# The moment matmuls of an output slot are moved from the slot's end to the place before the projection

## The chip, the cores and the metric

The kernel runs on one core of one Trainium2 chip. The time is the device time of one execution in microseconds (us). TensorE multiplies matrices and writes to PSUM; VectorE, ScalarE and GpSimd work element by element; SyncE issues DMAs. Each engine executes its own list of instructions in order, and engines wait for each other by semaphores that only count upwards.

## The reference

The model takes `x` of 16 images, 64 x 64 positions (4096 tokens), 128 channels in float32. Layer 0 is a group norm and a two-dimensional LSTM. Layer 1 is Nystrom attention with 8 heads and 64 landmarks over the tokens, and then a recurrence with a batch norm in front of it. What matters here is the end of the attention and what the recurrence needs of it:

```python
out = attn1 @ attn2_inv @ (attn3 @ v)            # per head
out = out + res                                  # res: a convolution of v along the tokens
t = t + (x + out @ w_out + b_out)                # x: layer norm of the tokens
t = t + _L1_ffn_ref(_ln_t(t), W, V, gamma, beta)

# in _L1_ffn_ref
Wx = einsum('bti,hi->bth', x, W); flat = Wx.reshape(B * T, H)
Wx = (Wx - mean(flat)) * rsqrt(var(flat) + BN_EPS) * gamma + beta
```

The mean and the variance of `Wx` go over all tokens of all images. The kernel gets them from the sums and the second moments of the normalised tokens, which are ready only when the last token has been through the attention.

## The kernel before, in words

The phases run one after another: group norm, LSTM, landmarks, pseudo-inverse, output, recurrence. The change touches the output phase (`output_phase`). It works on 16 images of 8 chunks (`NG`), 512 tokens each, one chunk to a slot: 128 slots. `each_image` calls an engine's `slot(b, c, ...)` for image `b` and chunk `c`; there is a `slot` per engine, and the order of the calls in it is that engine's order of work, written out by hand. There is no planner. The work on one chunk is spread over several slots, so a slot also handles chunks c+1 to c+3 (ahead) and c-1 to c-4 (behind).

TensorE's slot (L2229), in order:

- `scores(c)` (L2171, L2175): into four PSUM banks; it waits among others for ScalarE's copy of the last convolution, because `bank_conv` is one of the four
- `row_maxima(c+1, 0)` (L2152): the approximate scores of the first half of the next chunk into two banks; VectorE reduces each bank (`maxima`, L2355), and the second call waits for those reductions before it writes the banks again
- `project(c-3)` (L2211): the output projection, into `bank_x`
- `row_maxima(c+1, 1)` (L2152): the second half
- `weigh(c)` (L2185): waits for ScalarE's four exponentials (L2318)
- `queries(c+3)` (L2138), `turn_maxima(c+1)` (L2160), `convolve(b+1, c)` (L2197), `turn_convolved(c-2)` (L2205)
- `moments(c-4)` (L2224): 16 small matmuls of the normalised tokens `u` with themselves, summed in `bank_m` over all slots

VectorE's slot (L2399): the four reductions for chunk c+1 (L2355), `residual(c-3)` (L2366), which adds the projection to the base and takes layer norm statistics of the result (L2369, L2372), `reciprocals(c-1)` (L2386), `normalise(c-2)` (L2397), `add_convolved(c-2)` (L2380), `merge(c-1)` (L2391).

GpSimd's slot (L2099): `mask(c-1)` (L2073), `norm(c-3)`, `base(c-1)` (L2097). `norm` waits for the statistics of the residual, adds epsilon (L2082, here called the variance step), raises to the power -0.5 (L2084) and multiplies the residual by it into `u` (L2089, the product). `u` has two buffers, taken in turn. `norm(c-3)` is called in slot c, so its result is what `moments(c-4)` of slot c+1 reads. SyncE stores each `u` to the tensor `scaled` and moves the softmax sums to packed form and back (L1987, L1996, L2003).

ScalarE's slot (L2314): exponentials (L2318), half of the base scaling (L2302), copies of queries, weighed values and maxima (L2295, L2310, L2312, L2280, L2284), the copy of the convolution (L2289), the other half of the scaling.

After the last slot the remaining `project`, `turn_convolved` and `moments` calls run down one by one, and ScalarE copies `bank_m` out when all moments are done (L2343).

Of the kernel before, what the change touches and what calls it, by code (L numbers as in the profile page):

```python
# [1877 lines left out]
def output_phase(nc, sems, R, E, K, xnt, tokens, vals, recips, scaled):  # L1878


    with ExitStack() as ctx:
# [47 lines left out]
        def nth(b, c):  # L1929

            return NG * b + c + 1

        def wait(eng, name, count):

            if count > 0:
                eng.wait_ge(s[name], count)
# [13 lines left out]
        def follows(c, k, last):  # L1950

            return c + k < NG or not last

        def precedes(c, k, first):

            return c >= k or not first
# [171 lines left out]
        def _(pe):  # L2128
# [5 lines left out]
            def queries(b, c):  # L2134

                pe.wait_ge(*loaded(s_xl, *at(b, c)))
                wait(pe, "qc", nth(b, c) - 1)
                nc.tensor.matmul(bank_q[:, :], w[:, :], xnT[c % 4][:, :], start=True, stop=True).then_inc(s["qm"], 1)  # L2138

            def row_maxima(b, c, r, q):  # L2140

                if r == 0:
                    wait(pe, "ql", nth(b, c))
                    wait(pe, "setup", SETUP * (b + (c == NG) + 1))
                    wait(pe, "neg", nth(b, c) - 1)
                for k in range(2):
                    for half in range(2):
                        if k == 0:
                            wait(pe, "max", GT * (nth(b, c) - 1) + 2 * r + half - 1)
                        rows, heads = slice(LM * half, LM * half + LM), slice(PAIRS_H * half, PAIRS_H * half + PAIRS_H)  # L2150
                        token = P * (2 * r + k)
                        ml = nc.tensor.matmul(bank_l[half][:, 2 * P * k:2 * P * k + 2 * P], q_lp[c % 2][rows, token:token + P],  # L2152
                                              kb_lp[q][rows, heads, :].rearrange("c h l -> c (h l)"), start=True, stop=True)
                        if k == 1:
                            ml.then_inc(s["lp"], 1)

            def turn_maxima(b, c):
                wait(pe, "max", GT * nth(b, c))
                for k in range(GT):
                    mt = nc.tensor.matmul(bank_l[0][:, P * k:P * k + P], m1[:, k, :], E.ident_lp[:, :], start=True, stop=True)  # L2160
                mt.then_inc(s["mt"], 1)

            def scores(b, c, q):

                wait(pe, "neg", nth(b, c))
                wait(pe, "denc", 2 * (nth(b, c) - 1))
                wait(pe, "qc", min(nth(b, c) + 2, B * NG))
                wait(pe, "convc", min(NG + nth(b, c) - 1, B * NG))
                for g in range(PAIRS_H):
                    rows = slice(QUAD * g, QUAD * g + QUAD)  # L2170
                    nc.tensor.matmul(bank_s[g][:, :], ind[rows, :, :].rearrange("c a l -> c (a l)"), negm[c % 2][rows, :],  # L2171
                                     start=True, stop=False)
                for g in range(PAIRS_H):
                    rows = slice(QUAD * g, QUAD * g + QUAD)
                    ms = nc.tensor.matmul(bank_s[g][:, :], kb[q][rows, :, :].rearrange("c a l -> c (a l)"), qT[c % 4][rows, :],  # L2175
                                          start=False, stop=True)
                ms.then_inc(s["s1"], 1)

            def weigh(b, c, q):

                wait(pe, "exp", PAIRS_H * nth(b, c))
                for h in range(2):
                    rows = slice(LM * h, LM * h + LM)
                    for g in range(PAIRS_H):
                        mp = nc.tensor.matmul(bank_pv[h][QUAD * g:QUAD * g + QUAD, :], zb[q][rows, g, :], p1[g][rows, :],  # L2185
                                              start=True, stop=True)
                mp.then_inc(s["pv"], 1)

            def convolve(b, c, out):

                half, pair = c // GT, c % GT
                pe.wait_ge(s_v[half], 128 * (b + 1))
                turns = out.rearrange("p (n e) -> p n e", e=2 * DH)
                for a in range(2):
                    h = 2 * pair + a
                    for side in range(2):
                        mm = nc.tensor.matmul(turns[LM * side:LM * side + LM, :, DH * a:DH * a + DH], bands[:, h, :],  # L2197
                                              v[half][side][:, :, (DH + 1) * h:(DH + 1) * h + DH], start=True, stop=True,
                                              skip_group_check=True)
                mm.then_inc(s["conv"], 1)  # L2200

            def turn_convolved(b, c, q):
                wait(pe, "res", nth(b, c) - 1)
                for k in range(GT):
                    mt = nc.tensor.transpose(bank_x[:, k, :], res[q][:, GT * (c % NG) + k, :], R.ident[:, :])  # L2205
                mt.then_inc(s["ct"], 1)

            def project(b, c):
                wait(pe, "add", nth(b, c))
                for k in range(GT):  # L2210
                    mt = nc.tensor.matmul(bank_x[:, k, :], oT[:, P * k:P * k + P], wo[:, :], start=True, stop=True)  # L2211
                mt.then_inc(s["wo"], 1)

            def moments(b, c):

                n = nth(b, c)
                wait(pe, "u", n)
                if n == 1:
                    pe.wait_ge(K.ready, K.PARTS + 2)
                    wait(pe, "centre", 2)  # L2220
                for k in range(GT):
                    for g in range(P // QUAD):
                        r = (g - k) % BLOCK_ROWS
                        mm = nc.tensor.matmul(bank_m[QUAD * g:QUAD * g + QUAD, FROM[r]:FROM[r] + WIDTH[r]],  # L2224
                                              u[c % 2][:, k, 1 + QUAD * r:1 + QUAD * r + QUAD], u[c % 2][:, k, 0:WIDTH[r]],
                                              start=n == 1 and k == 0, stop=n == B * NG and k == GT - 1, skip_group_check=True)
                mm.then_inc(s["moments"], 1)

            def slot(b, c, q, first, last):  # L2229
                scores(b, c, q)  # L2230
                nq = q if c + 1 < NG else 1 - q
                if follows(c, 1, last):
                    row_maxima(b, c + 1, 0, nq)
                if precedes(c, 3, first):
                    project(b, c - 3)
                if follows(c, 1, last):
                    row_maxima(b, c + 1, 1, nq)
                weigh(b, c, q)
                if follows(c, 3, last):
                    queries(b, c + 3)  # L2240
                if follows(c, 1, last):
                    turn_maxima(b, c + 1)
                if not last:
                    convolve(b + 1, c, bank_conv[:, :])
                if precedes(c, 2, first):
                    turn_convolved(b, c - 2, q if c >= 2 else 1 - q)
                if precedes(c, 4, first):
                    moments(b, c - 4)

            nc.tensor.matmul(bank_m[:, 0:C], E.avg[:, :], fw[:, :], start=True, stop=True).then_inc(s["centre"], 1)  # L2250
            pe.wait_ge(s_band, 16)
# [8 lines left out]
            turn_maxima(0, 0)  # L2260
            wait(pe, "convc", NG)
            each_image(pe, slot)
            project(B - 1, NG - 3)
            turn_convolved(B - 1, NG - 2, 1)
# [594 lines left out]
```

## Time and profile before

| | |
|---|---|
| median of 3 runs | 5903.51 us (5903.4 to 5907.3) |
| the profiled execution, its own time | 5913.64 us |
| its span in the profile | 5911.8 us |
| TensorE matmuls busy | 5253.6 us, 89% |
| VectorE / ScalarE / GpSimd busy | 3071.2 (52%) / 3138.0 (53%) / 1523.0 (26%) us |
| scores of the output phase's first and last slot start | 2530.7 and 3561.8 us |
| last moment matmul starts | 3592.7 us |

The profile gives start and duration of each instruction on each engine. Engine names: PE is the matmul part of TensorE and PEld its weight loads, DVE is VectorE, ACT is ScalarE, POOL is GpSimd. Matmuls are pipelined, their ends are modelled and overlap the next start, so distances are best taken from start to start.

### The profile page before, as it was taken

The page shows a single profiled execution, that of the slowest core. Times are in us where ns is not written, and L with a number is a line of the kernel's source. Part 1 is how long each engine was busy: PE and PEld are TensorE (multiplying, and loading weights), DVE is VectorE, ACT ScalarE, POOL GpSimd, SP SyncE. Part 2 cuts the span into 40 slices and gives each one's busy share as a digit, 9 for nine tenths or more (in the row PEclk, how much of TensorE's full clock was granted, in tenths as well). Part 3 has the DMA queues.
Part 4 walks back from the last instruction along what each step waited for, and adds up shares of the span by engine and source line. Part 5 has one row for each costly group of instructions (what it writes and reads, how often), then busy time and mean ns, then how long its engine had stood idle before and what let it go on. Part 6 is the DMA issues. An engine that isn't in the chain of part 4 may idle for free. (4 is left out here: it accounts for less than half of the span.)

```text
span 5911.8 us, 223297 instructions
## 1 busy us (share of the span) xinstructions
PE 5253.6 (89%) x97395; PEld 3278.2 (55%) x97488; DVE 3071.2 (52%) x8152; ACT 3138.0 (53%) x9108; POOL 1523.0 (26%) x1905
## 2 busy tenths in 40 slices
PE   5599999997899998799999997888888888888888
PEld 4599888896566666744444444333333333333333
DVE  8677777775788886568888883111111111111111
ACT  6465555565677776378888883333333333333333
POOL 2100000002888874256666662000000000000000
PEclk7899999999999999999999998999999999999999
DMA  9631111225777773467777762111111111111100
GB/s 389 270 115 58 58 58 60 84 77 183 245 245 243 231 243 105 102 175 203 202 203 202 204 173 66 33 34 32 32 34 33 32 32 35 32 32 32 35 18 24
DMA packets 773031, 689.32 MB, mean 117 GB/s; under 512 B 67056, under 2 KB 663024, under 8 KB 767984
## 3 DMA queue, kind: packets, MB, share of 16 engines
q1 hardware_dynamic: 754672, 575.39, 32.6%
q0 software_dynamic: 14672, 95.16, 4.0%
q8 instruction: 743, 12.17, 0.9%
q10 hardware_dynamic: 2736, 4.89, 0.2%
q14 instruction: 208, 1.70, 0.1%
HBM read 392.17 MB, written 274.89 MB: 113 GB/s over the span
## 5 line engine op out<-in xcount | busy, mean ns | idle before, releaser
L2797 ACT ACTIVATE f_y<-f_acc 128x16 f32<-128x16 f32 x4096 | 754.7, 184 | 1542.5 <-PE f_acc L2739 1542.5
L2739 PEld LDWEIGHTS f_acc<-f_y,f_vT 128*32 128x32 f32 x32768 | 645.2, 108 | 1438.7 <-ACT f_y L2797 1437.0
L2739 PE MATMUL f_acc<-f_y,f_vT 128*32 128x16 f32 x32768 | 1046.1, 193 | 279.6 <-issue 1.5
L2697 PE MATMUL f_junk<-f_idle 128*32 128x512 bf16 x8400 | 832.5, 376 | 0.0
L2579 DVE COPY f_zT<-f_zt 128x512 f32<-128x512 f32 x124 | 85.8, 692 | 1138.4 <-PE f_zt L2653 1138.4
L2355 DVE TENSOR_REDUCE o_m<-o_bank_l 128x8 bf16<-128x512 f32 x512 | 329.7, 686 | 132.4 <-PE o_bank_l L2152 130.0
L2572 DVE TENSOR_SCALAR f_wxn<-f_wxp,f_scale,f_shift 128x512 f32<-128x512 f32 x126 | 102.1, 811 | 509.0 <-PE f_wxp L2667 508.9
L1299 ACT ACTIVATE a_p<-a_s 128x512 f32<-128x512 f32 x502 | 259.3, 602 | 153.0 <-PE a_s L1166 151.2
L2318 ACT ACTIVATE o_p<-o_bank_s 128x512 f32<-128x512 f32 x512 | 264.4, 602 | 142.0 <-PE o_bank_s L2175 142.0
L533 POOL DMA_DIRECT2D hidden<-l_h x46 | 34.7, 756 | 1162.1 <-DVE l_hsum L790 961.6
L712 ACT ACTIVATE l_gate<-l_pf,r_ctx 128x256 f32<-128x256 f32 (+7 forms) x512 | 202.5, 446 | 229.1 <-PE l_pf L643 228.8
L2592 DVE SCALAR_TENSOR_TENSOR f_sum<-f_u,f_std,f_turned 128x128 f32<-128x128 f32 x512 | 143.6, 344 | 317.9 <-PE f_turned L2690 317.9
L2697 PEld LDWEIGHTS f_junk<-f_idle 128*32 128x32 bf16 x8400 | 250.0, 99 | 0.0
L1359 DVE TENSOR_REDUCE a_m3p<-a_s 128x1 f32<-128x512 f32 x360 | 223.6, 684 | 50.8 <-PE a_s L1126 49.4
L633 PE MATMUL l_pio<-l_x,r_k_lm 128*128 128x256 f32 (+7 forms) x1024 | 239.0, 356 | 0.2 <-ACT l_gate L729 0.2
L633 PE MATMUL l_pf<-l_x,r_k_lm 128*128 128x256 f32 (+7 forms) x1024 | 238.9, 356 | 0.0
L647 PE MATMUL l_pio<-l_hsum,r_ctx 128*128 128x256 f32 (+7 forms) x1024 | 238.8, 356 | 0.0
L2302 ACT ACTIVATE o_base<-o_base,r_loss,r_gain 128x128 f32<-128x128 f32 x512 | 225.8, 498 | 0.3 <-DMA o_base<-tokens 0.3
L2690 PE MATMUL f_turned<-f_ident,f_y 128*32 128x128 f32 x4096 | 221.1, 290 | 0.5 <-DVE f_sum L2592 0.5
L1017 POOL TENSOR_TENSOR a_r<-a_vare,a_half 128x8 f32<-128x8 f32 x128 | 209.6, 1638 | 10.0
L712 ACT ACTIVATE l_gate<-l_pio,r_ctx 128x256 f32<-128x256 f32 (+7 forms) x512 | 203.4, 450 | 13.9
L2679 PE MATMUL f_acc<-f_wxn,f_ident 128*32 128x128 f32 x4096 | 207.1, 274 | 0.7 <-issue 0.7
(323 smaller groups left out, 11517.6 us busy)
## 6 DMA issues: line engine op xcount, KB each, us to landing
o_v<-vals SPq DMA_DIRECT2D x256, 272.0 KB, 3.4
a_hid<-hidden SPq DMA_DIRECT2D x112, 520.0 KB, 5.0
hidden<-l_h POOLq DMA_DIRECT2D x46, 1040.0 KB, 6.6
l_x<-skew SPq DMA_DIRECT2D x46, 1024.0 KB, 5.2
vals<-a_v SPq DMA_DIRECT2D x128, 272.0 KB, 3.4
gn_x<-in_x SPq DMA_DIRECT2D x16, 2048.0 KB, 17.4
a_xin<-in_x SPq DMA_DIRECT2D x128, 256.0 KB, 5.1
tokens<-a_t SPq DMA_DIRECT2D x128, 256.0 KB, 3.4
```

Source lines behind the costliest of these rows:

```text
L633: mm = nc.tensor.matmul(banks[c][g][:, :, rows], w[W[g]], xs, start=g in (0, 2, 3), stop=False, skip_group_check=True)
L647: mm = nc.tensor.matmul(banks[c][g][:, :, rows], w[U[g]], hsum[:, lanes[c], rows], start=False, stop=True, skip_group_check=True)
L712: nc.scalar.activation(gate[:, g, lanes[c], rows], banks[c][g][:, :, rows], ACT.Tanh if g == 2 else ACT.Sigmoid, bias=bias[BI[g]]).then_in ...
L1299: nc.scalar.activation(p3[c % 2][g][:, :], score_bank(i, c, g), ACT.Exp).then_inc(s["exp"], 1)
L1359: nc.vector.tensor_reduce(m3p[:, g, c:c + 1], bank[:, :], AX.X, ALU.max).then_inc(s["mx"], 1)
L2302: nc.scalar.activation(bs[c % 4][:, k, :], bs[c % 4][:, k, :], ACT.Identity, scale=R.gain[:, b, n:n + 1], bias=R.loss[:, b, n:n + 1]).then ...
L2318: nc.scalar.activation(p1[g][:, :], bank_s[g][:, :], ACT.Exp).then_inc(s["exp"], 1)
L2355: nc.vector.tensor_reduce(m1[:, 2 * r:2 * r + 2, LM * half:LM * half + LM].rearrange("p k (g r) -> p k g r", r=QUAD)[:, :, :, 0:2], bank_l ...
L2690: mt = nc.tensor.matmul(turned[g % 2][rows, b % 4, :], y[q][:, rows, b], ident[:, :], start=True, stop=True)
L2697: nc.tensor.matmul(junk[rows, :], idle[:, 0:QUAD], idle[:, :], start=True, stop=True)
L2739: mm = nc.tensor.matmul(acc[k % 2][rows, t, :], vT[:, rows], before, start=False, stop=True, skip_group_check=True)
L2797: nc.scalar.activation(y[q][:, step, :], acc[step // RC % 2][:, step % RC, :], ACT.Sigmoid).then_inc(s_y, 1)
```

## The change

In TensorE's slot the call of `moments(b, c - 4)` with its condition is moved from the end of the slot to the place between `row_maxima(b, c + 1, 0, nq)` and `project(b, c - 3)`. The moments are the same, for the same chunk, in the same order. The slots 0 to 3 of the first image have no moments, before and after. The run-down after the last slot is not changed.

```diff
@@ -2231,6 +2231,8 @@
                 nq = q if c + 1 < NG else 1 - q
                 if follows(c, 1, last):
                     row_maxima(b, c + 1, 0, nq)
+                if precedes(c, 4, first):
+                    moments(b, c - 4)
                 if precedes(c, 3, first):
                     project(b, c - 3)
                 if follows(c, 1, last):
@@ -2244,8 +2246,6 @@
                     convolve(b + 1, c, bank_conv[:, :])
                 if precedes(c, 2, first):
                     turn_convolved(b, c - 2, q if c >= 2 else 1 - q)
-                if precedes(c, 4, first):
-                    moments(b, c - 4)
```

## Rows read from the trace of the kernel before

**Rows 1.** One line of code (duration min/median/max, first to last start); busy us by window.
```profile
L2171 PE MATMUL o_bank_s<-o_negm,o_ind x512: 371/385/385, 2530.7 to 3561.8; 32*128 32x512 bf16 x171
...
core 0: us, PE busy (x) PEld busy (x) DVE busy (x) ACT busy (x) POOL busy (x), PEclk, DMA share, GB/s
2561.30:3561.80 1000.50, 965.24 (x11502) 493.65 (x11502) 827.18 (x2090) 825.77 (x1714) 671.32 (x673) 1.00 0.70 197
```
**Rows 2.** Timeline of TensorE in one slot: start us, duration us, work.
```profile
3003.58 0.40 PE L2171 MATMUL o_bank_s<-o_negm,o_ind 32*128 32x512 bf16 x4
...
3004.76 0.39 PE L2152 MATMUL o_bank_l<-o_kb_lp,o_q_lp 64*128 64x256 bf16 x4
3005.08 1.16 PE L2211 MATMUL o_bank_x<-o_wo,o_oT 128*128 128x128 f32 x8
3006.18 0.75 PE L2152 MATMUL o_bank_l<-o_kb_lp,o_q_lp 64*128 64x256 bf16 x4
3007.02 1.09 PE L2185 MATMUL o_bank_s<-o_p,o_zb 64*32 64x512 f32 x16
...
3009.33 1.10 PE L2197 MATMUL o_bank_s<-o_v,o_bands 128*64 128x256 f32 x8
...
3010.95 0.77 PE L2224 MATMUL o_bank_m<-o_u 128*32 128x33 f32 x32
3011.65 0.40 PE L2171 MATMUL o_bank_s<-o_negm,o_ind 32*128 32x512 bf16 x4
```
**Rows 3.** Timeline of VectorE in the same slot.
```profile
3005.19 1.29 DVE L2355 TENSOR_REDUCE o_m<-o_bank_l 128x8 bf16<-128x512 f32 x2 [0.80 <-PE o_bank_l L2152]
3006.86 1.29 DVE L2355 TENSOR_REDUCE o_m<-o_bank_l 128x8 bf16<-128x512 f32 x2 [0.38 <-PE o_bank_l L2152]
...
3009.73 0.38 DVE L2372 BATCH_NORM_AGGREGATE o_mv<-o_st 128x2 f32<-128x6 f32 x4
...
3011.11 0.69 DVE L2380 TENSOR_TENSOR o_oT<-o_att,o_bank_x 128x512 f32<-128x512 f32 x1 [0.22 <-DVE o_att L2397]
3011.72 0.74 DVE L2391 SCALAR_TENSOR_TENSOR o_att<-o_odd,o_keep,o_pvs 128x512 f32<-128x512 f32 x1
```
**Rows 4.** Timeline of GpSimd in the same slot.
```profile
3004.02 1.27 POOL L2089 TENSOR_TENSOR o_u<-o_t,k_rstd 128x512 f32<-128x512 f32 x1
...
3010.19 0.76 POOL L2082 TENSOR_TENSOR o_vare<-o_mv,o_eps 128x4 f32<-128x4 f32 x1 [2.67 <-DVE o_mv L2372]
3011.02 1.02 POOL L2084 TENSOR_TENSOR k_rstd<-o_vare,o_half 128x4 f32<-128x4 f32 x1
3012.12 1.24 POOL L2089 TENSOR_TENSOR o_u<-o_t,k_rstd 128x512 f32<-128x512 f32 x1
```
**Rows 5.** Timeline of ScalarE in the same slot.
```profile
3004.91 2.06 ACT L2318 ACTIVATE o_p<-o_bank_s 128x512 f32<-128x512 f32 x4 [1.14 <-PE o_bank_s L2175]
```
**Rows 6.** Timeline of TensorE from slot 3, which has no moments, to slot 4.
```profile
2559.40 1.13 PE L2197 MATMUL o_bank_s<-o_v,o_bands 128*64 128x256 f32 x8
...
2561.32 0.40 PE L2171 MATMUL o_bank_s<-o_negm,o_ind 32*128 32x512 bf16 x4 [0.20 <-ACT o_res L2289]
```
**Rows 7.** Timeline of GpSimd in slot 13, then GpSimd and TensorE at the phase's tail.
```profile
2634.11 0.76 POOL L2082 TENSOR_TENSOR o_vare<-o_mv,o_eps 128x4 f32<-128x4 f32 x1 [3.48 <-DVE o_mv L2372]
...
2636.05 1.07 POOL L2089 TENSOR_TENSOR o_u<-o_t,k_rstd 128x512 f32<-128x512 f32 x1
...
3589.14 0.20 POOL L2082 TENSOR_TENSOR o_vare<-o_mv,o_eps 128x4 f32<-128x4 f32 x1 [2.92 <-DVE o_mv L2372]
...
3590.51 1.04 POOL L2089 TENSOR_TENSOR o_u<-o_t,k_rstd 128x512 f32<-128x512 f32 x1
...
3591.60 0.76 PE L2224 MATMUL o_bank_m<-o_u 128*32 128x33 f32 x14 [3.70 <-POOL o_u L2089]
```
**Rows 8.** Waits of VectorE in 2561.3 to 3561.8: us in total, times, longest.
```profile
DVE o_rec_packed L2386 <- DMA o_den_packed<-o_odd: 30.5, 43, 2.2
```
**Rows 9.** Busy us by window (columns as in rows 1), tail and slot 28.
```profile
3574.00:3576.50 2.50, 2.24 (x36) 1.77 (x36) 1.71 (x10) 0.00 (x0) 1.15 (x2) 0.50 0.12 36
...
2758.00:2768.00 10.00, 8.60 (x112) 4.47 (x107) 8.94 (x21) 7.03 (x15) 6.28 (x7) 1.00 0.68 194
```

## The prediction, made before the changed kernel was run

> **What bounds the kernel now.** I read the page's share of the span first, then the output phase alone by windows, then one of its slots engine by engine, then the waits.
>
> The change touches only the output phase, 128 slots (16 images of 8 chunks). TensorE starts the scores of the first slot at 2530.7 us and of the last at 3561.8 us [rows 1]. The moments run from slot 4 on. From the scores of slot 4 (2561.3 us) to those of slot 127 there are 123 periods in 1000.5 us, a mean of 8.134 us, and TensorE is busy 965.24 us of them, 96%; VectorE and ScalarE 83%, GpSimd 67% [rows 1]. So TensorE's own queue sets the period, and a block of matmuls moved inside that queue is work neither saved nor added. What counts is which waits it moves past, and who waits for what then comes later.
>
> A usual slot starts its scores at 3003.58 us and the next at 3011.65, 8.07 us later. In between stand: first row maxima 3004.76, projection 3005.08, second row maxima 3006.18, weighing 3007.02, query projection, turned maxima, convolution 3009.33, turned convolution, moments 3010.95 [rows 2]. I call the start of a slot's scores S; these are S+1.18, +1.50, +2.60, +3.44, +5.75, +7.37.
>
> **What the change moves.** Sixteen matmuls with their weight loads and one wait (for `u` of chunk c-4) leave the end of the slot and stand at S+1.50, ahead of the projection. No instruction, byte or DMA is added or removed, and no other engine's list changes. The block takes 11.65 - 10.95 = 0.70 us of the queue [rows 2].
>
> *Its gain.* Two waits of TensorE shrink. The second row maxima wait for VectorE's reductions of the first: the reductions start at 3005.19 and take 1.29 us for two, so both end at 3006.48, while TensorE reached this point at 3006.18 [rows 2, 3]. The weighing waits for four exponentials that run 3004.91 to 3006.97 [rows 5], and starts at 3007.02. With 0.70 us more ahead of them both are ready: projection S+2.20, second maxima S+2.20+1.10 = S+3.30, weighing 0.32 us later (the spacing 3004.76 to 3005.08 of undisturbed maxima) = S+3.62 instead of S+3.44. The block thus costs 0.18 us there and leaves 0.70 at the end. But the end has a floor: scores wait until ScalarE has copied the convolution out. A slot before the moments begin shows it: convolution 2559.40, scores 2561.32, 1.92 us [rows 6]. So convolution at S+5.75+0.18 = S+5.93, next scores S+7.85. By TensorE and ScalarE alone a slot would fall from 8.07 to about 7.85.
>
> *Its cost.* The wait for `u` comes with the block. `u` of chunk c-4 is the last step of GpSimd's normalisation, and it isn't long finished: GpSimd runs it 3004.02 to 3005.29, that is to S+1.71 [rows 4]. At the old place (S+7.37) that left 5.7 us of slack; the new place is S+1.50. So the block waits, with TensorE's strict order behind it: projection, second maxima, weighing, everything. That would cost little (0.2 us) if `u` stayed at S+1.71, but `u` hangs on the very maxima queued behind the block. VectorE's list is: all four reductions of chunk c+1, then the residual of chunk c-3, its statistics, and from these GpSimd makes `u` of chunk c-3, for which the *next* slot's block waits. It is a ring of one turn per slot:
>
> - block to projection 0.70 [rows 2]
> - projection to second maxima 3006.18 - 3005.08 = 1.10 [rows 2]
> - second maxima to VectorE's third reduction: undisturbed as the first pair, 3005.19 - 3004.76 = 0.43 [rows 2, 3]
> - third reduction to GpSimd's first step: 3010.19 - 3006.86 = 3.33 (two reductions, residual, statistics) [rows 3, 4]
> - GpSimd: variance, power, product, from 3010.19 to the end of the product at 3012.12 + 1.24 = 3013.36, 3.17 here; from 2634.11 to 2636.05 + 1.07 = 2637.12, 3.01 in slot 13; from 3589.14 to 3590.51 + 1.04 = 3591.55, 2.41 at the phase's tail [rows 4, 7]
> - its end to the block's first matmul: 3591.60 - 3591.55 = 0.05 [rows 7]
>
> Without GpSimd that is 5.61 us; with its three figures the ring is 8.78, 8.62 or 8.02 us.
>
> Which GpSimd time? It depends on what VectorE runs beside it. The product takes 1.04 us alone, 1.24 beside the merge of VectorE (3011.72) [rows 3, 4, 7]. In the ring the merge comes earlier: its predecessor, the addition of the turned convolution, started at 3011.11 after 0.22 us of idle time [rows 3], for it also needs the turned convolution, which ends about then. In the ring the convolution starts 2.30 us after the weighing (3009.33 - 3007.02), so the turned copy is there early and VectorE runs on without the gap. That is the pattern of slot 13: variance 2634.11, product 2636.05 for 1.07 [rows 7]. I take 3.01. The short 2.41 appears where the reciprocals wait for their packing DMA and leave GpSimd alone; they wait 43 times in the 123 periods [rows 8]. With half a microsecond more per slot for that DMA chain I take 15 short ones. Mean period: 8.62 - 0.60 x 15/123 = 8.55 us.
>
> In the ring TensorE stands still 8.55 - 7.85 = 0.7 us a slot, in one gap ahead of the block. The other waits drown in it: first reductions end at S+2.90, second maxima start after S+4; the conv copy is awaited before the gap; the slots longer than 8.07 in the old stretch (its mean is 8.134), where a matmul waited for VectorE or a DMA elsewhere, lose their excess. In the last image, which has no convolution and runs shorter slots, the ring holds the period just the same.
>
> One rule I weigh apart, and the sum stands without it. The product beside the merge was released 1.24 - 1.04 = 0.20 us late, i.e. at 3012.32, 0.60 us after the merge began and 0.14 before its end [rows 3, 4]. The Trainium skill (SBUF — State Buffer, Who interferes with whom) says that a VectorE instruction with two SBUF inputs and a GpSimd one that reads SBUF exclude each other for the whole instruction, and that a `tensor_reduce` never contends. By the first half, a product that arrives at the merge would wait 0.15 longer than the rows show, some 0.15 x 123 = 18 us in all (an estimate by that page); the row speaks for the shorter lock. By the second half the next slot's reductions, which run beside the product in the ring, would not lengthen it; no row here tests that, and the bound of 8.78 below covers a product 0.16 longer.
>
> **The sum.** The first block (slot 4) waits for the `u` made from slot 3; the ring starts at once. Blocks of slots 4 to 127 are 123 turns of 8.55 = 1051.7 us. The block stands 2.2 us into its slot in the ring (1.50 + 0.7), and about as late in slot 4 already, where it waits for a `u` made on the old beat: no term for the start. The old stretch is 1000.5. Difference +51 us. The tail of the phase, 34 us, follows DMA and VectorE steps that don't move: 0, give or take 2. The recurrence phase behind it is shifted whole. The profiled execution takes 5913.64 us (span 5911.8), so it would be 5964.8; against the median of the runs shown, 5903.51, it is 5954.5. I say 5954.
>
> Bounds of the ring: all turns at 8.78 give 123 x 8.78 - 1000.5 = +79 (5983); a third of them short (8.42) gives +35 (5939); all short (8.02) is a rival below.
>
> **The rivals.**
> *The ring doesn't close, the gain stays.* If `u` were ready before S+1.50, the period would be 7.85: 123 x 7.85 - 1000.5 = -35 us, 5869. For it: both shrinking waits are real. Against: `u` ends at S+1.71 already in slots of 8.07, and shorter slots or later reductions only move it back. Chance 0.02.
> *GpSimd is always short (not slower).* If the shifted VectorE work leaves GpSimd alone from variance to product, the ring is 8.02: 123 x 8.02 - 1000.5 = -14 us, 5889. It decides from a GpSimd chain of 8.134 - 5.61 = 2.52 us downwards. For it: 2.41 exists. Against: reciprocals and the normalisation directly follow the statistics on VectorE, as they do in the slots with 3.0 and more. Chance 0.03 for this, 0.03 for a mixture that ends within 0.2% (mean ring 8.04 to 8.23).
> *The clock falls.* Standing still each slot could drop TensorE from 2.4 to 1.2 GHz; the phase's tail does show a granted 0.50 after longer stops [rows 9]. At half the clock block and projection take up to twice their 0.70 and 1.10 us: the ring grows by up to 1.8 us, by 123 x 1.8 = 221 us to about 6175. Against: ten microseconds with TensorE 14% idle (8.60 of 10.00 busy) kept the grant at 1.00 [rows 9]. The ring idles 8%. Chance 0.01.
> *The ring is long,* 8.78 or more: 5983 and above, chance 0.13. My forecast holds the remaining 0.78.
>
> **How the numbers follow.** About 0.2% (12 us) is what a measurement can tell from no change. Slower by more: 0.78 + 0.13 + 0.01 = 0.92; same 0.03; faster 0.02 + 0.03 = 0.05. The range runs from 5928 (mean ring 8.34, nearly half the turns short) to 5983 (all at 8.78).
>
> **What would show it.** Right: TensorE idle ahead of the moments, put down to GpSimd's product, about 0.7 us, 124 times; no wait left ahead of second maxima and weighing; TensorE's share in the phase near 91%; scores to scores near 8.6 in the first and the last image alike; block start equal to product end plus 0.05. Wrong: no such idle time and a period under 8.1; or a product that ends early; or a third reduction that no longer follows the second maxima at once.

## The result, and the profile after

The changed kernel took 5974.06 us, median of 4 runs (5968.05 to 5977.36), against 5905.41 us (5903.4 to 5914.07, 4 runs) for the kernel before beside it: ratio 1.0111, 95% interval [1.0095, 1.0127]. The forecast was 5954 in a range of 5928 to 5983, and slower with a chance of 0.92. It holds; it is 20 us low, and the parts of these 20 us are taken up below.

The profiled execution took 5975.4 us, its span is 5973.7, 61.9 more than before. The same first view as in [rows 1] shows where: one line of code by first and last start, then busy time by window from the scores of slot 4 to those of slot 127.

```profile
L2171 PE MATMUL o_bank_s<-o_negm,o_ind x512: 371/384/385, 2536.7 to 3625.5; 32*128 32x512 bf16 x171
...
core 0: us, PE busy (x) PEld busy (x) DVE busy (x) ACT busy (x) POOL busy (x), PEclk, DMA share, GB/s
2567.31:3625.46 1058.15, 938.85 (x11502) 487.83 (x11502) 811.67 (x2091) 826.93 (x1713) 660.80 (x674) 1.00 0.67 186
```

The stretch is 1058.15 us for 1000.50, +57.7. The count of matmuls is the same, 11502. TensorE was busy 96% of it and is now 89%. Its busy time fell by 26 us for the same matmuls (965.24 to 938.85); their ends are modelled, so the distances from start to start decide and not this sum. The first slot starts at 2536.7 for 2530.7: 6.0 us were lost ahead of anything that was changed. The rest of the span, behind slot 127, is 1.8 us shorter. 57.7 + 6.0 - 1.8 = 61.9. These are differences between two profiled executions, and that of the kernel before (5913.64 us) was among its longer ones: its medians in the experiments are 5906.81 to 5909.24.

The next view is the timeline of TensorE in one slot (start, duration, work), and answers to [rows 2].

```profile
3004.52 0.40 PE L2171 MATMUL o_bank_s<-o_negm,o_ind 32*128 32x512 bf16 x4 [0.20 <-ACT o_res L2289]
...
3005.70 0.39 PE L2152 MATMUL o_bank_l<-o_kb_lp,o_q_lp 64*128 64x256 bf16 x4
3007.07 0.77 PE L2224 MATMUL o_bank_m<-o_u 128*32 128x33 f32 x32 [0.97 <-POOL o_u L2089]
3007.77 1.16 PE L2211 MATMUL o_bank_x<-o_wo,o_oT 128*128 128x128 f32 x8
3008.86 0.39 PE L2152 MATMUL o_bank_l<-o_kb_lp,o_q_lp 64*128 64x256 bf16 x4
3009.18 1.09 PE L2185 MATMUL o_bank_s<-o_p,o_zb 64*32 64x512 f32 x16
...
3013.40 0.40 PE L2171 MATMUL o_bank_s<-o_negm,o_ind 32*128 32x512 bf16 x4 [0.20 <-ACT o_res L2289]
...
3015.65 0.77 PE L2224 MATMUL o_bank_m<-o_u 128*32 128x33 f32 x32 [0.67 <-POOL o_u L2089]
```

TensorE stands still ahead of the moments (0.97 and 0.67 us), for GpSimd's `u`, and at one other place only, 0.20 for ScalarE's copy. Block to block it is 3015.65 - 3007.07 = 8.58 us. VectorE and GpSimd in the same stretch, to set beside [rows 3] and [rows 4]:

```profile
3005.37 0.74 DVE L2391 SCALAR_TENSOR_TENSOR o_att<-o_odd,o_keep,o_pvs 128x512 f32<-128x512 f32 x1
3006.13 1.29 DVE L2355 TENSOR_REDUCE o_m<-o_bank_l 128x8 bf16<-128x512 f32 x2
3009.28 1.29 DVE L2355 TENSOR_REDUCE o_m<-o_bank_l 128x8 bf16<-128x512 f32 x2 [1.86 <-PE o_bank_l L2152]
...
3012.45 0.32 DVE L2386 RECIPROCAL o_rec_packed<-o_den_packed 128x32 f32<-128x32 f32 x1
3012.68 0.63 DVE L2397 TENSOR_TENSOR o_att<-o_att,o_rden 128x512 f32<-128x512 f32 x1
...
3013.95 0.74 DVE L2391 SCALAR_TENSOR_TENSOR o_att<-o_odd,o_keep,o_pvs 128x512 f32<-128x512 f32 x1
```

```profile
3004.04 1.57 POOL L2084 TENSOR_TENSOR k_rstd<-o_vare,o_half 128x4 f32<-128x4 f32 x1
3005.68 1.33 POOL L2089 TENSOR_TENSOR o_u<-o_t,k_rstd 128x512 f32<-128x512 f32 x1
...
3012.61 0.76 POOL L2082 TENSOR_TENSOR o_vare<-o_mv,o_eps 128x4 f32<-128x4 f32 x1 [3.37 <-DVE o_mv L2372]
3013.45 1.02 POOL L2084 TENSOR_TENSOR k_rstd<-o_vare,o_half 128x4 f32<-128x4 f32 x1
3014.54 1.05 POOL L2089 TENSOR_TENSOR o_u<-o_t,k_rstd 128x512 f32<-128x512 f32 x1
```

One turn can be read off, from the block at 3007.07: projection 0.70 later, second maxima 1.09, third reduction 0.42, variance step 3012.61 - 3009.28 = 3.33, end of the product 3015.59, 2.98 later, next block 0.06. The sum is 8.58. Over the whole stretch 123 of the 124 blocks start 0.05 to 0.06 us behind the end of a product; one stands 1.01 us behind it.

The waits of TensorE's weight loads, then of its matmuls, and those of VectorE, 2567 to 3616 (us in total, times, longest; the loads run ahead of the matmuls and meet `u` first):

```profile
PEld o_bank_m L2224 <- POOL o_u L2089: 121.8, 121, 1.9
```

```profile
PE o_bank_m L2224 <- POOL o_u L2089: 87.1, 114, 1.6
PE o_bank_s L2171 <- ACT o_res L2289: 23.6, 117, 0.2
```

```profile
DVE o_rec_packed L2386 <- DMA o_den_packed<-o_odd: 3.4, 7, 0.8
```

### The profile page after: what moved, and what is told of

It reads as the page before. It is cut to its first block and busy times, and to the rows that moved or that the text cites. A ratio compares the mean times of both kernels' runs of the same rounds, so it can differ in the third digit from the quotient of the medians.

```text
span 5973.7 us, 223297 instructions
## 1 busy us (share of the span) xinstructions
PE 5231.7 (88%) x97395; PEld 3277.1 (55%) x97488; DVE 3054.5 (51%) x8152; ACT 3138.5 (53%) x9108; POOL 1512.4 (25%) x1905
```

## The experiments

Twelve more runs follow; "stretch" is the first to the last start of L2171 in the profiled execution. The ratio is to the kernel before on the same chip, 95% interval; its median there was 5905.41 us beside the change, 5906.81 beside e1 to e4, 5908.91 beside e5 to e8, 5906.89 beside e9 and e10, 5909.24 beside e11 and e12.

| kernel | median us | ratio | stretch us |
|---|---|---|---|
| before | 5903.51 | 1 | 1031.1 |
| the change | 5974.06 | 1.0111 [1.0095, 1.0127] | 1088.8 |
| e1 the change again | 5967.60 | 1.0104 [1.0087, 1.0121] | 1087.3 |
| e2 same place, one chunk later | 5901.94 | 0.9988 [0.9979, 0.9998] | 1023.6 |
| e3 block behind the projection | 5898.56 | 0.9987 [0.9977, 0.9996] | 1012.2 |
| e4 half there, half at the end | 5900.94 | 0.9991 [0.9981, 1.0000] | 1020.6 |
| e5 change + longer GpSimd chain | 6133.88 | 1.0378 [1.0357, 1.0399] | 1250.5 |
| e6 before + longer GpSimd chain | 5907.59 | 0.9997 [0.9987, 1.0008] | 1025.1 |
| e7 change, GpSimd left alone | 5911.07 | 1.0003 [0.9992, 1.0013] | 1033.5 |
| e8 e3, packing first | 6010.13 | 1.0168 [1.0151, 1.0185] | 1129.1 |
| e9 e3 again | 5904.83 | 0.9992 [0.9983, 1.0001] | 1018.9 |
| e10 e3, v loads last | 6086.63 | 1.0305 [1.0291, 1.0319] | 1200.3 |
| e11 e3, v loads first | 6043.99 | 1.0239 [1.0225, 1.0253] | 1166.7 |
| e12 before, v loads first | 6049.73 | 1.0240 [1.0226, 1.0254] | 1172.7 |

### The change again

> The changed kernel again, beside the kernel before on the same chip. Its profiled slots 4 to 127 are 57.7 us longer than before, its run-down 1.8 us shorter; another 6.0 us lie ahead of the output phase, in the group norm and the landmarks, which the change doesn't touch. If these 6 us are chance of phases timed by DMAs, the difference is 56 us (ratio 1.0095) within some 5; if they belong to the change, 62 to 68 us again (1.0105 to 1.0115).

The medians differ by 60.8 us, which the first of the two expectations allows for (56, within some 5). Stretch 1087.3 us for 1088.8, waits of the moments for `u` 91.0 us for 87.1, but the first slot starts at 2528.6, even 2.1 earlier than in the profile of before. So the stretch repeats, and the 6.0 us ahead of it in the first profile don't: nothing ties them to the change.

### Where the block stands, and what it waits for

```diff
 # e2, against the change: the same place, the moments of one chunk later
-                if precedes(c, 4, first):
-                    moments(b, c - 4)
+                if precedes(c, 5, first):
+                    moments(b, c - 5)
 ...
             each_image(pe, slot)
+            moments(B - 1, NG - 5)
```
```diff
 # e3, against before: the same chunk, behind the projection
                     project(b, c - 3)
+                if precedes(c, 4, first):
+                    moments(b, c - 4)
                 if follows(c, 1, last):
                     row_maxima(b, c + 1, 1, nq)
 ...
-                if precedes(c, 4, first):
-                    moments(b, c - 4)
```
```diff
 # e4, against before: two of the four tiles behind the projection, two left at the end
                     project(b, c - 3)
+                if precedes(c, 4, first):
+                    moments(b, c - 4, range(2))
 ...
-                    moments(b, c - 4)
+                    moments(b, c - 4, range(2, 4))
```

In e4 `moments` also gets its tiles as an argument and tells of its end only behind the last one.

> Same place ahead of the projection, but the moments of chunk c-5 instead of c-4 (one more call in the run-down). Ring theory: u of c-5 was finished a whole slot ago, no wait, the ring has two slots per turn; period 7.85 us (floor: the copied convolution), 123 x 7.85 - 1000.5 = -35 us against before, about 5870, ratio 0.994. Rival A (the matmul block itself costs at that place, by a drained or differently tiled TensorE between bf16 maxima and fp32 projection): still about 8.6 us a slot, 5970. Rival B (VectorE or ScalarE can't follow a shorter slot): 8.07, 5905.

> Moments of c-4 between the projection and the second row maxima. Ring theory: the block still stands ahead of the second maxima, so the ring closes, but without the projection's 1.10 us: 0.70 + 0.42 + 3.33 + 2.98 + 0.05 = 7.48 us, under the floor of 7.85; u is ready 0.3 to 0.4 us before the block wants it. Period 7.85, about 5870, ratio 0.994. Rival C (any place ahead of the second maxima closes a ring longer than the old slot): slower than before, 5920 or more. Rival B: 5905.

> Half of the block (8 matmuls, 0.35 us) between projection and second maxima, half at the slot's end. The first half fills the wait for the first reductions, the weighing keeps its start at S+3.44 (exponentials), convolution S+5.75, the second half fills the wait for the copied convolution: next scores at S+7.75. 123 x 7.75 - 1000.5 = -47 us, about 5858, ratio 0.992. If the two halves cost more than one block (two switches of tiling), 7.85 to 7.95: 5870 to 5882.

All three take the ring away and the slow-down with it: 66 us in e2 (5967.60 to 5901.94) for matmuls that stand at the very place of the change and differ only in reading a `u` that is a slot older. So neither the place nor its neighbours cost the time; the wait for a fresh `u` does. A slot of e3 that nothing disturbs, TensorE's timeline:

```profile
2998.11 0.40 PE L2171 MATMUL o_bank_s<-o_negm,o_ind 32*128 32x512 bf16 x4 [0.20 <-ACT o_res L2289]
...
2999.62 1.16 PE L2211 MATMUL o_bank_x<-o_wo,o_oT 128*128 128x128 f32 x8
3000.71 0.77 PE L2224 MATMUL o_bank_m<-o_u 128*32 128x33 f32 x32
...
3001.74 1.09 PE L2185 MATMUL o_bank_s<-o_p,o_zb 64*32 64x512 f32 x16
...
3005.93 0.40 PE L2171 MATMUL o_bank_s<-o_negm,o_ind 32*128 32x512 bf16 x4 [0.20 <-ACT o_res L2289]
```

It takes 3005.93 - 2998.11 = 7.82 us (the prediction's floor: 7.85), weighing at S+3.63 (3.62). The median slot of the stretch is 7.89 us in e2, 7.85 in e3 and 7.91 in e4. For e4 7.75 was forecast; 7.91 is what was expected if two half blocks cost more than one, and this was not looked into. But the times of all three missed their forecasts (5870, 5870 and 5858) by 29 to 43 us. The mean of e3's slots 4 to 119 is 8.02 (8.18 in the kernel before), and the kernel gains 8 us, not the 35 that 7.85 in each slot would give. (By the stretch alone it would be 19 us; but the profiled execution of the kernel before was a long one, and e6, whose TensorE works through the same list, has 1025.1 for 1031.1.) What makes the other slots late stands in the waits of e3, of VectorE and then of TensorE's weight loads and matmuls, 2561 to 3560:

```profile
DVE o_rec_packed L2386 <- DMA o_den_packed<-o_odd: 43.4, 70, 2.1
```

```profile
PEld o_bank_x L2211 <- DVE o_oT L2380: 20.1, 41, 3.8
```

```profile
PE o_bank_s L2197 <- DMA o_v<-vals: 8.9, 9, 1.3
...
PE o_bank_m L2224 <- POOL o_u L2089: 2.8, 7, 0.4
```

VectorE's reciprocals wait for the packed sums (30.5 us in 43 waits before [rows 8]), everything behind them on VectorE moves back, and at the end of that row the projection waits. The lateness isn't spread evenly: 11 of the 13 slots over 8.3 us are those of chunk 0 or 4 of an image, in e9 14 of 20. A second chain of about one slot's length thus stands behind the first. Four of the last five experiments go after it.

### The length of the ring

```diff
 # e5 against the change, e6 against before: a power whose result nobody reads
                 pool.tensor_tensor(r, vare[:, :], half[:, :], ALU.pow).then_inc(s["pow"], 1)
+                pool.tensor_tensor(spare[:, :], vare[:, :], half[:, :], ALU.pow).then_inc(s_spare, 1)
+                pool.wait_ge(s_spare, n + 1)
```
```diff
 # e7 against the change: merge and normalisation on one column of 512
-                nc.vector.scalar_tensor_tensor(out=att[c % 2][:, :], in0=odd[c % 2][:, :], ...
+                nc.vector.scalar_tensor_tensor(out=att[c % 2][:, 0:1], in0=odd[c % 2][:, 0:1], ...
-                nc.vector.tensor_tensor(att[c % 2][:, :], att[c % 2][:, :], rden[c % 2][:, :], ...
+                nc.vector.tensor_tensor(att[c % 2][:, 0:1], att[c % 2][:, 0:1], rden[c % 2][:, 0:1], ...
```

> The changed kernel with one more power instruction of GpSimd (128x4, into a tile that nobody reads) between the power and the product: 1.02 us and 0.08 to its neighbour, in every slot. Ring theory: each turn grows by the whole 1.10 us, 8.58 to 9.68; 123 x 1.10 = +135 us against the changed kernel, about 6103 to 6110. Rival (u is merely late within its slot, or the block costs something on TensorE itself): GpSimd is 67% busy and takes it in its idle time, at most a few us.

> The same added instruction in the kernel before. Ring theory: there the block stands 5.7 us behind the product, the ring has 5.7 us of slack, and nothing changes: 5905, within 8. Rival (GpSimd's or VectorE's load as such sets the slot): here too some tens of us up.

> The changed kernel with VectorE's normalisation (L2397) and merge (L2391) on one column instead of 512, so those two full-width operations are left out of the computation. Theory: GpSimd's chain from variance to product takes 2.98 us in the ring only because of these two; alone it takes 2.42. Ring 8.58 - 0.56 = 8.02: 123 x 0.58 = -71 us against the changed kernel, about 5897. Rival (the GpSimd times are its own): 2.98 stays, 5968.

e5 and e6 carry the same GpSimd work. Behind the old place it costs nothing (0.9997 [0.9987, 1.0008]); in the ring it costs 166 us (6133.88 - 5967.60, on chips whose kernel before differs by 2 us), 1.35 us for each of 123 turns where 1.10 was put in, and 24 us more than the upper forecast of 6110. From block to block 82 of the 123 turns take 9.6 to 9.75 us, as expected (8.58 + 1.10 = 9.68). The surplus is slots like the first of these two, whose windows (columns as above) and, for the first, timeline of TensorE are:

```profile
2923.30:2934.40 11.10, 9.23 (x94) 4.55 (x94) 6.53 (x18) 6.68 (x15) 6.71 (x7) 0.85 0.53 152
2954.50:2964.20 9.70, 8.88 (x106) 4.42 (x106) 7.68 (x19) 7.39 (x16) 7.45 (x9) 1.00 0.60 171
```

```profile
2926.62 0.77 PE L2228 MATMUL o_bank_m<-o_u 128*32 128x33 f32 x32 [1.75 <-POOL o_u L2093]
2927.32 1.78 PE L2215 MATMUL o_bank_x<-o_wo,o_oT 128*128 128x128 f32 x8
2929.04 0.61 PE L2156 MATMUL o_bank_l<-o_kb_lp,o_q_lp 64*128 64x256 bf16 x4
2929.58 1.80 PE L2189 MATMUL o_bank_s<-o_p,o_zb 64*32 64x512 f32 x16
```

After a stop of 1.75 us the projection takes 1.78 us for 1.16 and the weighing 1.80 for 1.09; the granted clock of this slot is 0.85, that is, TensorE ran part of it at 1.2 GHz and the rest at 2.4. In a later slot, in the second window, it is 1.00. The clock falls 33 times between slots 4 and 127, and the turns that it touches take 29 us more than 9.67 each would give, all others together 2. So the surplus goes with the clock. The stop alone doesn't decide: 58 turns with a stop of 1.7 to 1.8 us run at a granted 1.00 throughout. From block to second maxima, which is in the ring, it is 2929.04 - 2926.62 = 2.42 us for 1.79; the longer weighing comes on top for this slot alone.

e7 shortens GpSimd's chain by leaving out most of two VectorE operations, so what it computes is not the model's result. The timeline of GpSimd in one of its slots:

```profile
3015.72 0.20 POOL L2083 TENSOR_TENSOR o_vare<-o_mv,o_eps 128x4 f32<-128x4 f32 x1 [3.36 <-DVE o_mv L2376]
3016.00 1.02 POOL L2085 TENSOR_TENSOR k_rstd<-o_vare,o_half 128x4 f32<-128x4 f32 x1
3017.10 1.04 POOL L2090 TENSOR_TENSOR o_u<-o_t,k_rstd 128x512 f32<-128x512 f32 x1
```

3018.14 - 3015.72 = 2.42 us instead of 2.98 (2.41 to 2.46 in all slots), and the median slot is 8.03 us. The 56 us that this takes off the changed kernel (5967.60 to 5911.07, again on two chips) are those in which GpSimd stood behind VectorE's work. The kernel stayed some 14 us over what was expected of it (5897): 20 slots took over 8.3 us, 20 us more in all than 8.03 each would give, and VectorE's reciprocals waited for their packed sums again (35.1 us in 46 waits). With the ring at 8.02 us the second chain shows itself.

### The second chain

Its turn: reciprocals (L2386), spread of them to DRAM (L1996, the tensor `recips`), broadcast back (L2003, for the normalisation), packing of the next chunk's sums (L1987), next reciprocals. Spread, broadcast and packing are DMAs that SyncE issues, with the loads of v between spread and broadcast.

```diff
 # e8, against e3: the packing ahead of v loads and broadcast
                     spread(b, c - 1)
+                pack(b, c)
 ...
                     broadcast(b, c - 1)
-                pack(b, c)
```
```diff
 # e10, against e3: v loads behind the packing
-                if c < GT and b + 1 < B:
-                    wait(sp, "conv", NG * (b + 1))
-                    load_v(b + 1, 1, c)
 ...
                 pack(b, c)
+                if c < GT and b + 1 < B:
+                    wait(sp, "conv", NG * (b + 1))
+                    load_v(b + 1, 1, c)
 ...
```
```diff
 # e11, against e3, and e12, against before: v loads ahead of the spread
+                if c < GT and b + 1 < B:
+                    wait(sp, "conv", NG * (b + 1))
+                    load_v(b + 1, 1, c)
 ...
                 if precedes(c, 1, first):
                     spread(b, c - 1)
 
-                if c < GT and b + 1 < B:
-                    wait(sp, "conv", NG * (b + 1))
-                    load_v(b + 1, 1, c)
 ...
```

> As e3 (moments between projection and second maxima), and SyncE issues the packing DMAs of chunk c right behind the spreading ones of c-1, ahead of the loads of v and of the broadcast. In e3 the undisturbed slots took 7.83 us as reckoned, but the mean was 8.02: the reciprocals wait 70 times for the packing DMA. Theory: a second ring, reciprocals, spread 1.14, v loads 1.2, broadcast 0.7, packing 1.1, landing 3.3, reciprocals 0.35, about 8.0 us; the reordering takes some 1.9 out of it, the slot falls to its floor: 123 x 7.84 - 1000.5 = -36 us against before, 5870. Rival (the lateness comes from the DMA queues' own load, not from the order of issue): as e3, 5898.

> The kernel of e3 once more, to see whether its small gain over the kernel before holds on other runs. Ring theory with a second limit (SyncE's chain of packing transfers, about 8.0 us a turn): the slot that nothing disturbs takes 7.83 us, some slots wait for the packed sums; 5898 give or take 5, ratio to before 0.9975 to 0.9992. Rival: the gain of e3 was chance of its chip and minute; then a ratio within 0.9995 to 1.0015.

> The block behind the projection, as in e3, and on SyncE the loads of v moved behind the broadcast and the packing DMAs of the same slot (the broadcast and the packing keep their order, other than in e8). If the turn of SyncE's transfers from one reciprocals to the next is what eats the gain of e3, taking the wait for the convolution and the v loads (some 1.0 us from issue to issue) out of that turn shortens it from about 8.0 to about 7.0 us: the waits of the reciprocals fall from 43 us to under 15, the mean slot from 8.02 to 7.87 or less, and the kernel takes 5875 to 5888. Rival 1: the v loads, now a microsecond later, make the convolution wait instead (8.9 us in e3): 5895 to 5910 with these waits over 30 us. Rival 2: the excess of e3's slots comes from the chip's memory and not from the order of issue: unchanged, 5898 give or take 5, and the reciprocals still wait about 40 us.

> The block behind the projection, as in e3 and e9, and on SyncE the loads of v moved ahead of the spread of the reciprocals, where SyncE waits anyway (86.1 us in e9's stretch for the reciprocals and 86.4 us for the last broadcast to land); so the v loads come earlier than in e9, and they leave the turn of the packing transfers. Second-limit theory: with about 1.0 us less between spread and broadcast the waits of the reciprocals fall from 42 us to under 20 and the waits for v from 11 us to 0; mean slot 7.9, 5880 to 5893. Rival: the broadcast waits for the spread to land and not for SyncE (in e10, without the v loads between the two, it waited 2.5 us a slot), so nothing leaves the turn, and the spread's packets now run behind those of v: reciprocals wait as long as before or longer, 5898 to 5925.

> The kernel before with only the v loads moved ahead of the spread. The matmul queue holds its period at 8.07 us in a usual slot whatever SyncE does; its stretch from slot 4 to 127 has a mean of 8.134, so at most 0.06 x 123 = 8 us are to be had: second-limit theory 5898 to 5907. Rival (the spread runs late behind v): 5908 to 5930.

e9 repeats e3 with a little less gain: 0.9992 [0.9983, 1.0001] lies at the edge of what was expected, and its interval reaches into the rival's (chance). The changes of order on SyncE (e8, e10, e11, e12) were expected to help or to do little, and each made things much worse: 6010, 6087, 6044 and 6050 us where 5870, 5875 to 5888, 5880 to 5893 and 5898 to 5907 were forecast, and 110 to 180 us above what their rivals allowed. In e8 the reciprocals no longer wait, but the normalisation does, for the broadcast. In e10 26 convolutions wait for v, which its first rival had named with 30 us. VectorE's waits in e8 and TensorE's in e10:

```profile
DVE o_att L2397 <- DMA o_rden<-recips: 140.1, 103, 3.5
```

```profile
PE o_bank_s L2197 <- DMA o_v<-vals: 130.4, 26, 6.4
```

In e11 it is the spread, as its rival said. SyncE's rows of one slot (SPq marks the issue of a DMA), in e9 and then in e11:

```profile
3391.19 1.14 SPq L1996 DMA_DIRECT2D recips<-o_rec_packed  x2
...
3392.37 1.01 SPq L1553 DMA_DIRECT2D o_v<-vals  x2
...
3393.57 0.63 SPq L2003 DMA_DIRECT2D o_rden<-recips  x1
```

```profile
2839.53 1.35 SPq L1553 DMA_DIRECT2D o_v<-vals  x2
2840.99 1.15 SPq L1996 DMA_DIRECT2D recips<-o_rec_packed  x2
...
2844.76 0.62 SPq L2003 DMA_DIRECT2D o_rden<-recips  x1
```

From spread to broadcast it is 2.38 us in e9, with two loads of v issued in between, and 3.77 in e11, with nothing in between. Over slots 4 to 118 the medians are 2.39 and 4.31 us; in e12 it is 4.21 for 2.40 in the kernel before. The broadcast waits for the two small spreads to land, and they land later when the loads have been issued just ahead of them. The waits for it in the two kernels, SyncE, 2561 to 3560, e9 first:

```profile
SPq L2003 <- DMA recips<-o_rec_packed: 24.5, 30, 2.4
```

```profile
SPq L2003 <- DMA recips<-o_rec_packed: 327.3, 107, 4.2
```

e12 does the same to the kernel before, in which TensorE's own queue was the bound, and takes 1.0240 [1.0226, 1.0254]: its stretch grows by (1172.7 - 1031.1) / 127 = 1.1 us a slot, where spread to broadcast grew by 1.8. So the second chain of the kernel before had less slack than that. How much can't be read off, for TensorE's clock is in the sum: from slot 4 to 127 it is granted 0.95 in e12, 0.92 in e10, 0.98 in e11 and 0.99 in e8, where the kernel before, e3 and e9 have 1.00. What part of these four losses is the clock's was not taken apart.

That the broadcast's part of this chain is set by the landing of the spread is shown, and that lengthening it lengthens the slot; that the whole turn is about 8.0 us is reckoned and fits e3's waits, but was not measured turn by turn. Why a given slot of e3 is late and the next isn't (its slow slots take 8.3 to 10 us beside others of 7.82) was not taken apart. Nor does any kernel here remove the second chain, so whether the 35 us are to be had at all stays open. None beats the kernel before by more than 0.13%, and the best of them, e3, can't be told from the kernel before in its repetition, e9.

## Why the prediction was right

*The wait moves to `u`, and it closes a ring.* Shown: TensorE stands still ahead of the block for `u` (114 waits of its matmuls, 121 of its weight loads), and 123 of 124 blocks start within 0.06 us of the product's end. e2 takes only the ring away (the same place, older data) and the loss is gone. e6 and e5 lengthen GpSimd's chain outside and inside the ring: nothing, and at least the full amount.

*The ring's terms.* 0.70, 1.10, 0.43, 3.33 and 0.05 were measured as 0.70, 1.09, 0.42, 3.33 and 0.06. For GpSimd 3.01 was taken and 2.98 found: the product takes 1.05 and not 1.07. The choice of the pattern of slot 13 [rows 7] was right, since the merge comes early enough.

*The short turns* were put at 15; 7 GpSimd chains were short, and 6 of their turns were (8.02 to 8.06 us), since one block then stood a microsecond behind its product. The reason given was that the DMA chain gains half a microsecond a slot; it does, and more than was reckoned with: the reciprocals' waits fell from 43 to 7. This is the first mis-sized term: 3.3 us were gained where 9 had been taken off, some 6 us more.

*Long turns* had no term in the sum, though the range held them. 16 turns have a GpSimd chain of 3.09 to 3.29 us, some 4 us in all. The first rows of VectorE's and GpSimd's fences above show one: the power takes 1.57 instead of 1.02 and the product 1.33 instead of 1.05, since VectorE's row arrived a little later and lies over both; its slot is 8.88 us long. Some 3 us more lie in turns that were longer elsewhere (the block just named, four turns with GpSimd's first step 0.3 late). The usual ring of 8.58 for 8.62 takes 5 us back.

*The mean* was 8.60 for 8.55, +57.7 us for +51. From block to block the 123 turns sum to 1058.8 us for 1051.7; these 7 us are the four differences above (6 + 4 + 3 - 5) within their rounding. The mechanism was right; that the sum came within 7 us is helped by the ring's 5 us, which happen to stand against the other terms. The other 6.0 us of the 61.9 lie ahead of the stretch and didn't come back in e1. Of e1's median of 5967.60, which is 14 us above the forecast, its own stretch (1056.7 us from slot 4 to 127) explains 5, and 3 are the base (before had 5906.81 beside it, not 5903.51); 5 to 6 are left unexplained, with runs that spread over 12 us. The forecast took its old stretch of 1000.5 from an execution that was 7 us longer than that median; e6, with the same order of calls, has 994.5 for it, so some of the rest may lie there. This isn't shown.

*The last image* runs on the ring: its blocks stand 8.58 us apart but for two (8.86 and 8.99), where most slots took 6.5 to 7.3 us before. *The tail*: everything behind slot 127 changed by -1.8 (0 give or take 2). *The start* had no term, and block 4 stood at S+2.19 (2.2).

*The clock* was given 0.01, as a rival of all slots. It did not fall in the slots of the images with a convolution. It fell once, in the last image, where the stop ahead of the block is 2 us. TensorE's timeline of slot 126:

```profile
3619.27 0.77 PE L2224 MATMUL o_bank_m<-o_u 128*32 128x33 f32 x32 [2.07 <-POOL o_u L2089]
3619.97 1.35 PE L2211 MATMUL o_bank_x<-o_wo,o_oT 128*128 128x128 f32 x8
...
3621.80 1.96 PE L2185 MATMUL o_bank_s<-o_p,o_zb 64*32 64x512 f32 x16
...
3625.49 0.40 PE L2171 MATMUL o_bank_s<-o_negm,o_ind 32*128 32x512 bf16 x4 [0.74 <-ACT o_negm L2284]
```

The slot took 9.87 us for 8.58. But this is no cost of the change: in e1 the same slot took 8.58, and the kernel before has such a fall in its last image too, in slot 124 (10.03 us), where TensorE stopped 1.19 us and twice more for a short time:

```profile
3541.06 1.16 PE L2211 MATMUL o_bank_x<-o_wo,o_oT 128*128 128x128 f32 x8 [1.19 <-DVE o_oT L2380]
...
3543.30 1.96 PE L2185 MATMUL o_bank_s<-o_p,o_zb 64*32 64x512 f32 x16
```

e5 shows how near that rival was: with a ring a microsecond longer the clock fell 33 times.

*The rival "the gain stays"* reckoned 7.85 a slot and 35 us. e3 shows its slot (7.82) and not its time (8 us). Its premise, that nothing but TensorE's queue and ScalarE's copy bounds a slot, was wrong: the row of the packing waits [rows 8] was read as a supply of short turns only, and not as a sign of a second chain just below the old period. It didn't enter the forecast, since the ring was longer than both. *The other signs:* TensorE's share came out at 89% and not near 91%, since its busy time by the modelled ends fell; ahead of the weighing no wait is left, and ahead of the second maxima one of 0.3 us.

*The Trainium skill's rule* (SBUF — State Buffer, Who interferes with whom) was weighed for the product beside the merge. In the slot shown the merge ends at 3014.69 and the product starts at 3014.54 and takes 1.05 for 1.04 alone: the trace speaks for the shorter lock. The second half of the rule, that a `tensor_reduce` doesn't contend, agrees: the pair of reductions that ran beside the product (3006.13) took 1.29 us, and so did the pair that began with GpSimd idle (3009.28). Both read PSUM.

## What to carry to other kernels

When work is moved ahead in an engine's strict order, follow its input back through the other engines until either a point with slack or the moved work itself turns up; in the second case the slot's period is the length of that ring, whatever the engine's own work adds up to (as long as that is shorter), and giving the same work input one step older is the cure (66 us here). And before a gain is promised from taking the longest chain away, look for the next one: an engine that waits now and then, for a few tens of microseconds in all, for a transfer chain that turns once a slot (43 waits here) may mean that the chain is nearly as long as the slot.

## What was not expected of the hardware

- GpSimd behind VectorE: GpSimd's instruction ended as if it had been let go 0.14 us before the end of VectorE's. This holds within 0.01 us for each of the 154 instructions of its chain (variance step, power, product) that took over 0.1 us more than alone in the kernel before, and for each of the 128 in the changed one. The variance step at 3012.61 took 0.76 us beside reciprocals and normalisation and 0.20 alone (e7), so it was let go at 3013.17, and the normalisation ended at 3013.31. The product at 3005.68 took 1.33 for 1.04, let go at 3005.97; the merge ended at 3006.11.
- TensorE's granted clock fell in slots of 11 and 10 us after stops of 1.75 us (e5) and 2.07 us (the last image), though TensorE was busy 9.23 of the 11.1 us of that slot, and came back within it. In e5 58 turns with the same stop kept 1.00; in the kernel before it fell once after a stop of 1.19 us and two short ones.
- Two small transfers (8 KB each) issued by SyncE right behind loads of 272 KB each held up the broadcast that waits for them by 1.4 us in the slot shown (3.77 us for 2.38) and by 1.9 in the median (4.31 for 2.39), and this order alone makes the kernel before 2.4% slower (e12).
